# Preparing the sums of W2 beside the attention: f16 halves made per batch, loaded whole into the feed forward part, and the splits of x four slots earlier

## What is computed

```python
q = (query @ Wq + bq).reshape(b, s, N_HEADS, D_K).transpose(0, 2, 1, 3)
k = (key @ Wk + bk).reshape(b, s, N_HEADS, D_K).transpose(0, 2, 1, 3)
v = (values @ Wv + bv).reshape(b, s, N_HEADS, D_K).transpose(0, 2, 1, 3)
scores = jnp.einsum('bhqd,bhkd->bhqk', q, k) / jnp.sqrt(jnp.float32(D_K))
allowed = j < i + mask                      # mask == 0: row 0 attends to nothing
attn = jax.nn.softmax(jnp.where(allowed, scores, NEG_INF), axis=-1)
attn = attn.at[:, :, 0, :].set(0.0)
ctx = jnp.einsum('bhqk,bhkd->bhqd', attn, v)
x = layer_norm(query + ctx @ Wo + bo, ln1_g, ln1_b)
ffn = jax.nn.relu(x @ W1 + b1) @ W2 + b2
out = layer_norm(x + ffn, ln2_g, ln2_b)
```

## Time and profile before

| | us |
|---|---|
| median of 3 runs (lowest to highest) | 2691.99 (2690.86 to 2694.91) |
| the profiled execution, its own time | 2697.03 |
| its span | 2695.2 |
| mean granted clock of TensorE in it | 0.986 of full |
| PE busy | 2609.8 (97%) |
| DVE busy | 2106.7 (78%) |
| ACT busy | 1523.3 (57%) |
| POOL busy | 1558.6 (58%) |

### The profile page before, as it was taken

The page is one execution under the profiler, slowest core; times in us unless marked ns, Lnnn a source line. Parts: engine busy times, 40 slices in busy tenths (PEclk is TensorE's granted clock), DMA queues, the critical chain, the costliest instruction groups (busy, mean ns, idle before and its releaser), DMA issues.

```text
span 2695.2 us, 62128 instructions
## 1 busy us (share of the span) xinstructions
PE 2609.8 (97%) x22540; PEld 2238.6 (83%) x22540; DVE 2106.7 (78%) x5171; ACT 1523.3 (57%) x2945; POOL 1558.6 (58%) x1721
## 2 busy tenths in 40 slices
PE   7999999999999999977999999999999999999998
PEld 5888888888888888756888888888888888888887
DVE  6889889888888988978776767676767676767675
ACT  4777777777777777767444444444444444443443
POOL 3777777766666666655555454555454545454543
PEclk9999999999999999987999999999999999999999
DMA  6556555655555555555323232323232322222220
GB/s 193 149 148 160 148 144 146 158 150 143 150 139 135 138 138 134 140 135 160 92 51 68 51 68 51 68 51 68 51 69 51 68 53 66 54 65 55 65 55 26
DMA packets 439556, 273.35 MB, mean 101 GB/s; under 512 B 299648, under 2 KB 334400, under 8 KB 439248
## 3 DMA queue, kind: packets, MB, share of 16 engines
q1 hardware_dynamic: 438288, 267.79, 40.0%
q10 hardware_dynamic: 960, 1.57, 0.3%
HBM read 109.86 MB, written 57.67 MB: 62 GB/s over the span
## 4 chain that ended last, share of the span: by engine, by line
PE 82%; DVE 9%; issue 4%; POOL 2%; SPq 1%; DMA 1%; ACT 1%; ACTq 0%; DVEq 0%; POOLq 0%
PE h_ps L1361 24%; PE acc L1377 21%; PE lin_ps L700 9%; PE front L1347 6%; PE lin_ps L696 5%; PE max_ps L675 5%; PE st_ps L722 4%; PE o_ps L742 3%; DVE max_ps L656 2%; PE o_ps L744 2%; POOL prob_lo L421 2%; PE st_ps L757 2%; DVE xT L508 1%; DVE V L627 1%; DVE W L1268 1%
## 5 line engine op out<-in xcount | busy, mean ns | idle before, releaser
L421 POOL TENSOR_TENSOR prob_lo<-probs,prob_hi 128x512 f16<-128x512 f32 (+1 forms) x768 | 787.9, 1041 | 400.3 <-ACT prob_hi L500 398.5
L1361 PE MATMUL h_ps<-x_halves,W 128*128 128x256 f16 x6144 | 756.2, 273 | 0.8 <-ACT hf L1175 0.8
L1377 PE MATMUL acc<-W,hs 128*128 128x256 f16 x5376 | 669.6, 273 | 1.0 <-DVE hs L1321 1.0
L1361 PEld LDWEIGHTS h_ps<-x_halves,W 128*128 128x128 f16 x6144 | 596.3, 98 | 86.5 <-issue 15.9
L1175 ACT ACTIVATE hf<-h_ps,b1s,scale_evac 128x256 f32<-128x256 f32 x512 | 284.5, 562 | 593.1 <-PE h_ps L1361 591.3
L656 DVE CUSTOM_DVE_ANT_0 max_ps<-max_ps,mask_q 128x128 f32<-128x128 f32 (+3 forms) x1024 | 485.9, 504 | 134.6 <-PE max_ps L675 122.9
L1377 PEld LDWEIGHTS acc<-W,hs 128*128 128x128 f16 x5376 | 525.9, 98 | 62.2 <-issue 1.4
L498 ACT ACTIVATE probs<-st_ps 128x512 f32<-128x512 f32 (+1 forms) x768 | 406.6, 529 | 278.1 <-PE st_ps L757 241.1
L1101 POOL TENSOR_TENSOR hf<-hf 128x256 f32<-128x256 f32 x256 | 237.7, 929 | 503.2 <-ACT hf L1175 502.7
L500 ACT ACTIVATE prob_hi<-st_ps 128x512 f16<-128x512 f32 (+1 forms) x768 | 407.9, 531 | 0.0
L1321 DVE TENSOR_TENSOR hs<-hf,hs 128x896 f16<-128x896 f32 x256 | 276.9, 1101 | 141.1 <-ACT hs L1164 141.0
(11 more groups left out here) (119 smaller groups left out, 3795.9 us busy)
## 6 DMA issues: line engine op xcount, KB each, us to landing
heads<-stage SPq DMA_DIRECT2D x756, 128.0 KB, 2.4
raw<-in_xT SPq DMA_DIRECT2D x64, 256.0 KB, 3.1
o_in<-ctx_rows SPq DMA_DIRECT2D x256, 64.0 KB, 2.5
x_in<-in_x SPq DMA_DIRECT2D x32, 512.0 KB, 3.9
x_rows<-x SPq DMA_DIRECT2D x64, 256.0 KB, 2.1
o_in<-x_rows SPq DMA_DIRECT2D x256, 64.0 KB, 2.4
out<-y SPq DMA_DIRECT2D x32, 512.0 KB, 3.1
raw<-in_cT SPq DMA_DIRECT2D x60, 256.0 KB, 3.9
```

Of the source, the lines that this page charges most:

```text
L421: pool.tensor_tensor(prob_lo[:, k % 4, 0:w], probs[:, k % PROBS, 0:w], prob_hi[:, k % 4, 0:w], ALU.subtract).then_inc(pl_done, 1)
L1361: last = pe.matmul(h_ps[:, f % 2, 0:T], W1[:, aw, j, f * P:(f + 1) * P], x1_halves[:, item.parity, aa, j, :], start=(j == 0 and m == 0), s ...
L1377: last = pe.matmul(acc_products[:, n, :], hs[:, p % HS, aa, n, :], W2[:, p, aw, n, :], start=(p == 0 and m == 0 and n % 2 == 0), stop=(p = ...
```

## The change

Five things are done:

- **Moves in the attention's slots.** `X_LOAD` goes from 28 to 27 and `X_SPLIT` from 37 to 33 (the first batch keeps 37, through `x_splits`); `SCAN_LOAD` from 42 to 39, `SCAN_LOOK` from slot 50 to 46, `MIX` from 46 to 43. The gathering of the maxima and the scales follow the look, four slots earlier. On SP the loads of x now stand ahead of the heads' moves of the same slot.
- **A scale per row.** In batches 0 to 7 four tiny operations of DVE follow each look (L609, L611, L614, L617 of the new file): a power of two for each row of the pair of tiles, kept in `row_power`.
- **Halves.** ACT makes the high f16 half of the seven blocks with that scale (`HALF_HI`, 128x768 in slot 51 and 128x1024 in slot 58), DVE the low half (`HALF_LO`, slots 51 and 59), and SP stores both (`HALF_STORE`, slots 52 and 60, four transfers to a batch), ahead of the heads' moves of the same slot. The low halves are written in place over `raw`.
- **Loads whole.** In the feed forward part W2 is no longer staged and split. Eight transfers of 128x3584 f16 on ACT's queue, in feed slots 10, 11, 13, 15, 20, 21, 23 and 25, bring the halves straight into `W2`. The 16 chunks of W1 are split one to a slot, slots 5 to 20.
- **Scales of h.** Three more tiny operations of DVE in feed slot 5 fold the rows' powers into `h_evac` and `b1s`.

```diff
@@ the constants
-    X_LOAD = 28
-    X_SPLIT = 37
+    X_LOAD = 27
+    X_SPLIT = 33
+    FIRST_X_SPLIT = 37
...
-    SCAN_LOAD = 42
-    SCAN_LOOK = SLOTS + 2
-    MIX = SLOTS - 2
-    MIX_STORE = SLOTS + 11
+    SCAN_LOAD = 39
+    SCAN_LOOK = SLOTS - 2
+    MIX = SLOTS - 5
+    HALF_HI = (SLOTS + 3, SLOTS + 10)
+    HALF_LO = (SLOTS + 3, SLOTS + 11)
+    HALF_STORE = (SLOTS + 4, SLOTS + 12)
@@ SP, after the loads of x
+                for g, at in enumerate((slice(4, 7), slice(0, 4))):
+                    for item, _ in due(window, s, SLOTS, B, HALF_STORE[g]):
...
+                        for part, ready in ((0, bounds.half_hi), (1, bounds.half_lo)):
+                            wait_for(sp, ready, 2, item, g + 1)
+                            sp.dma_start(bounds.w2_halves[:, item.n, part, at, :], parts[g][1 + part]
+                                         ).then_inc(bounds.halves_stored, 16)
@@ ACT
+                for g in range(2):
+                    for item, _ in due(window, s, SLOTS, B, HALF_HI[g]):
...
+                        act.activation(hi, src, ACT.Copy, scale=bounds.row_value[:, 1:2]).then_inc(bounds.half_hi, 1)
@@ DVE, after the look
+                    if item.n < bounds.pairs:
...
+                        dve.tensor_scalar(value, bounds.part[:, :], 1e-12, None, ALU.max).then_inc(bounds.row_step, 1)
+                        dve.wait_ge(bounds.row_step, 4 * item.n + 1)
+                        dve.tensor_scalar(power.bitcast(U32), value.bitcast(U32), 0x7F800000, None, ALU.bitwise_and
+                                          ).then_inc(bounds.row_step, 1)
+                        dve.wait_ge(bounds.row_step, 4 * item.n + 2)
+                        dve.reciprocal(value, power).then_inc(bounds.row_step, 1)
+                        dve.wait_ge(bounds.row_step, 4 * item.n + 3)
+                        wait_for(dve, bounds.half_hi, 2, item, 0)
+                        dve.tensor_scalar(scale, value, SUM_TOP, None, ALU.mult).then_inc(bounds.row_step, 1)
+                for g in range(2):
+                    for item, _ in due(window, s, SLOTS, B, HALF_LO[g]):
...
+                        wait_for(dve, bounds.half_hi, 2, item, g + 1)
...
+                        dve.scalar_tensor_tensor(out=lo, in0=src, scalar=bounds.row_value[:, 1:2], in1=hi,
+                                                 op0=ALU.mult, op1=ALU.subtract).then_inc(bounds.half_lo, 1)
@@ the feed forward part
+    W2_LOAD = (10, 11, 13, 15, 20, 21, 23, 25)
+
     def split_slot(n):
 
-        return n if n < KT else PROJ + (n - KT) * 2 // 3
+        return n if n < KT else PROJ + n - KT
@@ ACT, in the feed forward part
+                for p in range(PAIRS):
+                    if (window, s) == (W2_LOAD[p] // SLOTS, W2_LOAD[p] % SLOTS):
+                        act.wait_ge(*(before.heads_read + [before.o_read])[heads_group(p)])
+                        act.wait_ge(bounds.halves_stored, 64 * PAIRS)
...
+                        act.dma_start(W2[:, p, :, :, :], bounds.w2_halves[:, p, :, :, :]).then_inc(w2_loaded[p], 16)
@@ PE, in the feed forward part
                     if item.n == 0 and half == 0:
-                        pe.wait_ge(w_lo, w2_chunks(p))
+                        pe.wait_ge(w2_loaded[p], 16)
```

More of the change, by code:

```diff
@@ L265, in attention, with x_splits @@
     o_out = sem("o_out")
+    def x_splits(window, slot, j, behind=0):
+        rest = after_first(due(window, slot, SLOTS, B, X_SPLIT + 2 * j + behind))
+        first = due(window, slot, SLOTS, 1, FIRST_X_SPLIT + 2 * j + behind)
+        return [item for item, _ in (*rest, *first)]
     def chunk_of(kind, j):
@@ L427, in gpsimd @@
                             continue
-                        block = raw[:, :, :].rearrange("p i (h n) -> p (i h) n", n=256)
+                        block, _ = bounds.mixes(raw)
                         if n == 0:
@@ L613, in vector @@
                         split(item, "c", j)
-                    for item, _ in due(window, s, SLOTS, B, X_SPLIT + 2 * j + 2):
+                    for item in x_splits(window, s, j, 2):
                         split(item, "x", j)
@@ L894, in feed @@
     HALVES = ((0, 1, 2, 3), (4, 5, 6))
+    BLOCK = (0, 3, 1, 2, 4, 5, 6)
     HS = 4
@@ L942, in feed @@
     w_lo = sem("w_lo")
-    b1_scaled = sem("b1_scaled")
+    w2_loaded = [sem(f"w2_loaded{p}") for p in range(PAIRS)]
+    h_scales = sem("h_scales")
     bv_hi = sem("bv_hi")
@@ L1010, in part_of @@
     def part_of(n, part):
-        if n >= KT and order[n - KT][0] == "w2":
-            return chunks[n][1][part]
         return chunks[n][1][:, part, :]
-    def raw_of(n):
-        if n >= KT and order[n - KT][0] == "w2":
-            return raw_slot(n).rearrange("p (h n) -> p h n", h=2)
-        return raw_slot(n)
     def weights_due(window, slot, behind=0):
@@ L1028, in feed @@
     scale_w1, scale_w2, scale_x1, scale_h = (bounds.scale[:, n:n + 1] for n in range(4))
-    h_evac, y_evac, y_less = bounds.evac[:, 0:1], bounds.evac[:, 3:4], bounds.less[:, 0:1]
-    weight_scale = [None] * KT + [{"w1": scale_w1, "w2": scale_w2}[w] for w, _ in order]
+    y_evac, y_less = bounds.evac[:, 3:4], bounds.less[:, 0:1]
     acc_products = acc[:, :, :].rearrange("p b (h n) -> p (b h) n", h=2)
@@ L1145, in scalar @@
                         act.wait_ge(bounds.ready, 2)
-                    if n >= KT and order[n - KT][0] == "w2":
-                        act.wait_ge(*(before.heads_read + [before.o_read])[heads_group(order[n - KT][1])])
                     if n < KT:
```

106 lines of the change are left out of this document (66 added, 40 removed).

## The result

The changed kernel takes 2699.7 us (median of 20 runs, 2695.1 to 2705.5), the kernel before 2691.7 us (20 runs, 2688.2 to 2699.4). The ratio is 1.0025, with an interval from 1.0018 to 1.0032: slower by 0.25%, some 7 us by the ratio and 8 us between the medians, where 2686 us was forecast.

A forecast was written before the change was run, and what follows sets the result against it. PE was taken as the bound, busy 97% of the span, with some 20 us to win in the transition. Terms -12 + 9.1 - 2.4 + 1.5 - 2 = -5.8 us, about 6, took 2692.0 to 2686 us; range 2673 to 2701 us.

The forecast's parts named there:

- -12 forecast: Transition from attention to feed forward: 12 us less, from fewer DVE splits, fewer PE waits and a fuller clock; bounds 4 to 24.
- I cost the loads at nothing: Transition: W2's loads cost nothing, with two slots of slack per pair and some 25 us between load and use.
- Rival C: Transition gives only 4 us, PE's waits passing to ACT behind W2's transfers, clock unchanged; 2694 us; chance 0.18.
- 10 splits x 1.1 us: Transition: 10 weight splits leave DVE, booked as 3.3 us in slots 5 to 9 and 5.1 us in the other seven.
- the 2.8 us booked for the clock: Transition: a denser stretch keeps more of PE's full clock; a quarter of at most 11 us taken, 2.8 us less.
- +9.1 forecast: Seven W2 batches in the attention: 1.3 us more each from tiny operations, low halves and stores, 9.1 us more (1.4 to 21).
- The stall behind the look: W2's batches: the second unit's maxima come 1.3 us later against a 0.4 us margin, so PE stalls 0.9 us.
- rival B: W2's batches: port lock and delayed stores make tiny operations and low half dear, 3.4 us a batch; 2701 us; chance 0.22.
- -2.4 forecast for eight: Eight W1 batches in the attention: 0.3 us less each (0.7 less to 0.1 more), 2.4 us less in all.
- 0.1 lost there and 0.3 lost where two more splits now stand: W1's batches: losses at the second unit's maxima and at the moved x splits, set against 0.7 us won at `onorm`.
- +1.5 forecast: Start-up: look, tiny operations and halves of batch 0 come into an unfilled pipeline, 1.5 us more (0 to 3).
- -2 forecast: Block of scales at the attention's end: four slots sooner, SP's chain starts sooner; 2 us less (4 less to 1 more).

The follow-up runs named there:

- e15: Kernel before, with the second tiny DVE operation for a group's rows replaced by a one-operand one writing zeros: 2692.6 us, ratio 0.9999.
- e3: Changed kernel with the fold of the maxima and the four tiny operations three slots behind the look: 2684.9 us, ratio 0.9964.
- e10: Changed kernel with the fold in its place, written as a tensor_scalar with the running maximum as its scalar: 2691.6 us, ratio 0.9983.
- e5: e3 with W2's loads cut to one of seven blocks per pair, which PE reads for all seven products: 2676.7 us, ratio 0.9941.
- e11: Changed kernel with the fold later in W2's batches alone, x_in loaded ahead of context rows, W2's loads in feed slots 18 to 32: 2677.9 us, ratio 0.9930.
- e8: e7 with x_in loaded ahead of the context rows' transfers, in every chunk of tokens but the first: 2668.0 us, ratio 0.9905.
- e13: e12 with x_in loaded early, as in e6 and e8: 2661.4 us, ratio 0.9885.
- e12: Kernel before with x alone moved (X_LOAD 27, X_SPLIT 33, loads ahead of heads' moves), look and sums as before: 2662.7 us, ratio 0.9872.
- e7: e1 with the fold of the maxima three slots behind the look: 2670.0 us, ratio 0.9913.
- e14: e11 with DVE's low halves four columns wide for 256, and the high halves stored in their place: 2668.7 us, ratio 0.9911.
- e2: Changed kernel with W2's eight loads in feed slots 16, 18, ... 30: 2700.9 us, ratio 1.0018.
- e4: Changed kernel with each W2 load cut in two, one piece in each feed slot from 10 to 25: 2704.1 us, ratio 1.0036.
- e6: e3 with x_in loaded ahead of the context rows' transfers, in every chunk of tokens but the first: 2679.9 us, ratio 0.9954.
- e1: Kernel before with only the moves of the attention's slots; W2 sums in f32 and 44 chunks split as before: 2678.6 us, ratio 0.9940.

## Why the prediction was wrong

The sign was wrong, and so was most of the sum. The two large errors, 13 us too good in the transition and 12 us too bad in the batches of W1, nearly cancel; what is left of the miss by the stages is 8 us in start-up and scales, so that the total came within 14 us of the forecast is in part luck. "Before" is here the mean of the kernel before and e15, which have the same work in these stages but for one operation of 0.18 us.

**The transition: -12 forecast, about +1 measured** (129.8, 129.5 and 130.1 us in after, e3 and e10, for 128.1 and 129.1). Three steps failed. "I cost the loads at nothing", since each pair has slots enough before its use, looked at who waits for W2 and not at who shares the transfers: W2's loads slow `x_rows`, `o_in` and the rows' moves of the heads on the chain, and cost 6.6 us (e5). Rival C had named this, with the price of no gain. Second, 10 splits x 1.1 us were booked as PE's by DVE's busy share. Measured, the splits give 4.0 us (e11 against e8 and e13, all with x_in early) to 5.2 us (e5 against before, where e5 also leaves out bytes that the kernel before does load), not 12. The chain there runs for much of its length through transfers and SP's issues, and splits taken off DVE don't shorten those. Third, the 2.8 us booked for the clock: it stayed at 0.75, 0.59 and 0.84, for 0.73, 0.59 and 0.83, and from 1260 to 1280 us it was 0.88 where it had been 1.00. There about as many matmuls (147 for 146) kept PE busy for 19.32 us instead of 17.63, so the clock, if anything, cost more where a gain was counted.

**Batches of W2: +9.1 forecast, +4 to +15 measured** (513.9, 519.4 and 520.3 for 510.3 and 505.6; +9.9 by the means). The size is about right and the parts are not. x's move gives 12 to 17 us here (e12), which I had at 0.3 each. The look in slot 46 alone takes 4.9 back (e7), the halves with the fold out of the way 8.4 (e3), of which the low ones on DVE are 1.0 of 1.2 us a batch (e14), and fold and tiny operations behind the look another 7 to 14 (after, e2 and e4 against e3). The stall behind the look was forecast at 0.9 us, in W2's batches alone; it came there alone, and measured 0.6 to 2.3. The port's lock struck, but I laid it on the four tiny operations, which took 0.14 to 0.17 us every time, and not on the fold in front of them, which was there before, took 0.16 to 0.24 us in its old place, and met POOL in its new one. The Trainium skill's "SBUF — State Buffer", section "Who interferes with whom", has this wait for two SBUF inputs; the fold's 1.11 us, ending with POOL's instruction, agree. The low halves, which have two SBUF inputs too, took 1.02 to 1.21 and 1.28 us for my 0.94 and 1.26: the extra 1 us of rival B is not there.

**Batches of W1: -2.4 forecast for eight, -14.3 measured for seven** (494.3 us for 507.6 and 509.6). The step that failed is the loss I set against the gain: "0.1 lost there and 0.3 lost where two more splits now stand", and before it the stall of 1.14 us read as the x split's 0.84 us. The chain in front of that stall held 0.61 + 1.08 us of two tiny operations for 0.16 + 0.18; with x gone none of them takes over 0.3 us in W1's batches (12 did before), and PE waits 0.1 us in all seven for 9.3. Everything of the stall, and the stretch behind it, was to be had: 2.0 us.

**Start-up: +1.5 forecast, about +5 measured** (108.2 to 109.5 us for 102.7 and 104.3). Batch 1's look is in it, with its wait of 2.3 us; with the fold later it is 103.3 to 107.0 us (e3, e5, e6, e11), and e14, without DVE's whole low halves, has 103.4 for e11's 107.0.

**Scales: -2 forecast, +2 measured** (68.8 to 69.6 for 66.2 and 67.3). PE's wait for the rows' moves fell from 7.8 to 5.9 us, as forecast. But the block of scales has only changed its victim: before, it stood between maxima, where PE waited 3.0 us; four slots sooner it fills DVE from 1115.2 to 1120.6 us ahead of the output of a head, and PE waits 3.75 us for its `onorm` at 1122.58 us. e12, with the scales where they were, has 69.2 too, so this is not the whole of it; what sets the stage is open.

By the means of the traces with the same work these stages add up to 5.3 + 9.9 - 14.3 + 2.4 + 1.2 = 4.5 us, with a scatter of some us between executions; 7 us were measured.

Rival B, the slower side, had its time right to about 1 us (2701), in part by luck: its own parts (0.7 for the tiny operations, 1 for the low half, 0.7 for the stores) make 3.7 us a batch and not 3.4, 2703 us. Its mechanism was half right: the lock was dear, but in the fold. The fourteen batches together got 4.4 us shorter by the means, start-up and scales took that back, and it was the transition that gave nothing, as in C.

x's move is worth 2.0 us in a batch where the wait it removes is 1.14. A comparison of the 4480 matmuls of W1's seven batches, step by step, before and in e12, says where: 1.6 us a batch at two products of `o_ps` 3 us apart (the second is the one of the 1.14 us wait), the rest in delays of 0.3 us and less in the projections and scores right behind them. The excess of the rows' operations, 21.3 - 3.0 = 18.3 us over 14 batches, is 1.3 us of it. How much of the 2.0 us is this excess and how much the split's own 0.84 us is not shown, since e15 could not take the wait away.

## What to carry to other kernels

A tiny DVE operation can be dear where POOL works: if its form waits, it costs the rest of POOL's instruction, and when it is on a chain that PE waits for, its place, or a form that doesn't wait, is worth more than its length; look at min and max, not at the median. A transfer hidden from its own user still has a price for the short ones it shares the engines with; ask which of those are on the chain that ends last. And a change of several parts should be run part by part: here one part, x four slots sooner, was worth 1.3%, and the others took more than that back.

## What the runs showed of the hardware

- The fold, a DVE operation of 128x1 with two SBUF operands, took 159 to 1117 ns in the changed kernel; the long ones (over 450 ns, there and in e1 to e4 and e7) all ended 0.01 to 0.02 us behind a POOL instruction. As a tensor_scalar with the second operand as its scalar it took 212 to 216 ns in all 16 cases.
- One operand is not enough to be free of this. A tensor_scalar of 128x16 took up to 1090 ns in e15 and waited for POOL like the two-operand form. In the changed kernel one of 128x4 (L570) took 0.90 us, one of 128x8 (L1279) 0.88 us and those of 128x2 (L1243) up to 0.49 us, each ending within 0.03 us of a POOL instruction. None with a single column did: all 300 tensor_scalars of 128x1 in the 17 traces took 140 to 216 ns, and 111 of them began beside a POOL instruction that had over 0.2 us to run. So it is neither the output's type nor the kind of scalar alone; that the number of columns decides is the plain reading, and no run varied it by itself.
- A reciprocal of 128x2 never waited: 149 to 168 ns in 1105 cases, 1033 of them beside POOL.
- Beside loads of 896 KB (917,504 bytes) on another queue the two first 256 KB transfers `x_rows` took 5.2 and 7.2 us, for 2.1 and 2.5 us before, and a 4 KB move of rows 5.0 us, for 2.2 us elsewhere on the chain. Cutting the loads in two didn't help (e4).
